# The third gate weight summed by ScalarE and rounded by GpSimd, and the next batch's input of the second attention in eight transfers

## The chip, the cores and the metric

One core of a Trainium2 chip. The metric is the device time in microseconds of one execution, in the median of several.

## The reference, cut to what matters

Two layers over the same 4 x 1024 tokens of width 256. Each takes a layer norm, an attention, and a gate network whose output, through silu, multiplies the attention's. The change touches the second layer alone: its gate network (the third weight, `w3`) and the order in which its attention loads its input.

```python
def _quantize(w):
    gamma = jnp.mean(jnp.abs(w))
    return jnp.clip(jnp.round(w / (gamma + 1e-08)), -1.0, 1.0)

x1 = x @ _quantize(w1).T            # w1, w2: 704 x 256, w3: 256 x 704
x2 = x @ _quantize(w2).T
hidden = jax.nn.sigmoid(x1) * x2
g = _silu(hidden @ _quantize(w3).T)

q, k, v = x @ Wq.T, x @ Wk.T, x @ Wv.T    # 32 heads of 64, rotary positions on q and k
# 30 heads look at the current block of 128 and the 64 rows before it, 2 heads at all rows before
x = x + (attention(q, k, v) @ Wo.T + bo) * g
```

## The kernel before

One program for all five engines, written out by hand: each stage has a plan, a Python list of steps, and every engine walks the same list and issues its own part of each step, in that order. An engine never overtakes: what waits holds back all that stands behind it on that engine. The stages before the change (the first layer, some 1460 us) aren't touched.

**The gate network** (`gate_network_plan`, `gate_network`) works on eight chunks of 512 tokens. A chunk has six steps `hidden` of 128 hidden units. TensorE makes two products into two PSUM banks (L1319, L1320: eight matmuls of 128x512 a step), ScalarE takes the sigmoid of the first (L1284, `n_sg`), VectorE multiplies (L1394, `n_hf`), ScalarE copies it rounded to the product's format (L1288, `n_hdh`), VectorE subtracts that for the low part (L1398, `n_hdl`, from `n_hf` and `n_hdh`). The steps share four banks, so the products of a step wait for the sigmoid and the multiply of the step two before. Beside them runs the front of the next chunk: `sums` on VectorE (L1350, L1353 and the variance L1355), the power -1/2 of it on GpSimd (L1252, `n_rs`), `begin` on VectorE (L1362, `n_xn`, which needs `n_rs`), and the transposes `turn0` and `turn1` on TensorE (L1305, they need `n_xn`). From the second chunk on, two steps `tail` (L1330, L1331) multiply the chunk before it by the rounded third weight `n_f3`.

The third weight, 128 x 1536 numbers a core (`n_raw3`), is rounded in a step `quantize` behind the first `hidden` of the second chunk, all of it on VectorE: the sum of the absolute values (L1374), a product with ones on TensorE that adds it over the partitions (L1311), the threshold (L1377, L1380, L1382), the comparison below (L1385) and the one above minus the first (L1387). The first attention rounds the other two weights, 128 x 1408 each, in another way: their sum is one ScalarE instruction (L1011), their rounding three GpSimd instructions (L982, L984, L986).

**The second attention** (`second_attention_plan`, `second_attention`) has 64 turns, 16 for each of the four batches of 1024 tokens. A turn handles two heads in two strides (the 16th of a batch, with the two global heads, in eight short ones). A stride begins with the scores on TensorE (L1921). Beside a turn's attention run the projections of the next turn (L107 to L109), for which the weights come in two turns ahead. All transfers are issued by SyncE, one after the other, in this order within a turn: the four `earlier` (L1734 to L1737, copies of values between partitions), `load_x` or `load_gx` if there is one, `load_w` (L1708 for q, L1709 for k), every other turn `load_v` (L1713), then the `rope` transfers (L1745, 16 a turn). `wo` (L1750, 512 KB, every fourth turn), and the stores and fetches of the output (L1758, L1768, L1769) lie ahead of `earlier`. ScalarE rounds the weights that have come in a step `w_high` (L1834), which waits for both of `load_w`; behind it in ScalarE's queue is a copy of values out of PSUM (L1846, `b_vv`) that frees a bank which the next scores (L1921) need.

`load_x` is two transfers of 1 MB (L1719): for the second batch in turn 1, for the third in turn 15, for the fourth in turn 31. In turn 47 `load_gx` (two of 1 MB) brings what the last batch's output is multiplied by and added to. Turns are counted from 0.

## Time and profile before

| | us |
|---|---|
| median of 3 runs | 3141.9 |
| lowest and highest of them | 3138.3, 3142.72 |
| the profiled execution's own time | 3153.16 |
| its span, first to last instruction | 3151.3 |
| PE busy | 3018.0 (96%) |
| DVE busy | 2118.1 (67%) |
| ACT busy | 1862.7 (59%) |
| POOL busy | 1013.5 (32%) |

The mean granted clock of TensorE is 0.985 of full speed. The profiled execution took 11 us more than the median of the others; sums are made against its time. "L1834" is a line of the kernel before; PE is TensorE, DVE VectorE, ACT ScalarE, POOL GpSimd, SPq the queue on which SyncE issues transfers. The gate network runs from 1460 to 1632 us, the second attention from there to the end.

### The profile page before, as it was taken

The page shows a single profiled execution, that of the slowest core. Times are in us where ns is not written, and L with a number is a line of the kernel's source. Part 1 is how long each engine was busy: PE and PEld are TensorE (multiplying, and loading weights), DVE is VectorE, ACT ScalarE, POOL GpSimd, SP SyncE. Part 2 cuts the span into 40 slices and gives each one's busy share as a digit, 9 for nine tenths or more (in the row PEclk, how much of TensorE's full clock was granted, in tenths as well). Part 3 has the DMA queues.
Part 4 walks back from the last instruction along what each step waited for, and adds up shares of the span by engine and source line. Part 5 has one row for each costly group of instructions (what it writes and reads, how often), then busy time and mean ns, then how long its engine had stood idle before and what let it go on. Part 6 is the DMA issues. An engine that isn't in the chain of part 4 may idle for free. (4 is left out here: it accounts for less than half of the span.)

```text
span 3151.3 us, 66387 instructions
## 1 busy us (share of the span) xinstructions
PE 3018.0 (96%) x23638; PEld 2264.8 (72%) x23638; DVE 2118.1 (67%) x5888; ACT 1862.7 (59%) x4638; POOL 1013.5 (32%) x1627
## 2 busy tenths in 40 slices
PE   7999999999999999997988999999999999999999
PEld 5888888853444444444877888788887888788887
DVE  5666666678999989984755555655556555565556
ACT  4666666647877777774445555455554555545553
POOL 0000000001100000001016566576655766566653
PEclk9999999988999999998999999999999999999999
DMA  4111111231332232202324434354343543344431
GB/s 150 48 48 48 48 48 41 61 69 31 81 48 55 46 73 35 42 4 89 115 59 111 104 94 99 96 128 103 84 117 87 119 103 93 93 115 110 97 89 44
DMA packets 296483, 246.35 MB, mean 78 GB/s; under 512 B 148956, under 2 KB 231516, under 8 KB 296028
## 3 DMA queue, kind: packets, MB, share of 16 engines
q1 hardware_dynamic: 296156, 242.11, 31.2%
q8 instruction: 191, 3.13, 0.4%
q14 instruction: 136, 1.11, 0.1%
HBM read 100.71 MB, written 44.04 MB: 46 GB/s over the span
## 5 line engine op out<-in xcount | busy, mean ns | idle before, releaser
L1853 ACT ACTIVATE b_pp<-b_pp,b_nm 128x192 f32<-128x192 f32 (+2 forms) x1024 | 472.9, 463 | 452.8 <-DVE b_nm L2020 371.3
L176 DVE TENSOR_REDUCE mx<-ps 128x2 f32<-128x1024 f32 x512 | 622.4, 1224 | 64.4 <-PE ps L167 51.9
L1007 ACT ACTIVATE a_pt<-ps 128x512 f32<-128x512 f32 x1024 | 555.9, 595 | 185.3 <-PE ps L1043 184.3
L1823 POOL TENSOR_SCALAR b_pp<-b_pp,b_rc 128x192 f32<-128x192 f32 x960 | 387.0, 425 | 384.8 <-DVE b_rc L2029 384.8
L2041 DVE COPY b_pt<-ps 128x384 f32<-128x384 f32 (+2 forms) x336 | 181.9, 555 | 317.1 <-PE ps L1942 301.8
L2020 DVE CUSTOM_DVE_ANT_0 b_pp<-ps,b_mk 128x192 f32<-128x192 f32 x960 | 276.3, 353 | 134.9 <-PE ps L1921 134.9
L797 DVE SCALAR_TENSOR_TENSOR f_yac<-ps,f_cw,f_yac 128x128 f32<-128x128 f32 x992 | 277.9, 343 | 125.4 <-PE ps L596 123.0
L596 PEld LDWEIGHTS ps<-w,f_sq 128*128 128x128 f32 x2048 | 265.1, 191 | 26.5 <-issue 6.0
L596 PE MATMUL ps<-w,f_sq 128*128 128x128 f32 x2048 | 270.1, 275 | 0.3
L1976 PE MATMUL ps<-b_wo,b_oT 128*128 128x256 f32 x1024 | 241.6, 380 | 3.7 <-ACT b_vv L1846 3.7
L1056 PE MATMUL ps<-a_pt,a_v 128*32 128x256 f32 x3072 | 242.9, 396 | 0.0
L1942 PE MATMUL ps<-ident,b_pp 128*128 128x128 f32 x1440 | 234.2, 273 | 2.7 <-DVE b_qp L1998 2.5
L990 POOL TENSOR_TENSOR a_s<-a_s,g 128x256 f32<-128x256 f32 x32 | 23.4, 730 | 573.9 <-DVE a_s L1114 573.9
L1921 PE MATMUL ps<-b_kp,b_qp 64*128 64x192 f32 x1920 | 189.9, 337 | 18.0 <-ACT b_vv L1846 10.2
L1976 PEld LDWEIGHTS ps<-b_wo,b_oT 128*128 128x128 f32 x1024 | 185.3, 190 | 25.3 <-ACT b_vv L1846 4.4
L1942 PEld LDWEIGHTS ps<-ident,b_pp 128*128 128x128 f32 x1440 | 177.8, 141 | 34.2 <-issue 3.7
L490 ACT ACTIVATE rl<-ps 128x512 f32<-128x512 f32 x256 | 151.7, 593 | 80.0 <-PE ps L109 75.5
L1846 ACT ACTIVATE b_vv<-ps 128x256 f32<-128x256 f32 x256 | 97.5, 381 | 169.1 <-PE ps L109 168.8
L1921 PEld LDWEIGHTS ps<-b_kp,b_qp 64*128 64x128 f32 x1920 | 154.7, 188 | 56.3 <-issue 56.3
L1995 DVE TENSOR_TENSOR b_qf<-ps,xt 128x512 f32<-128x512 f32 x256 | 174.2, 681 | 29.5 <-PE ps L109 29.5
L1853 ACT ACTIVATION_READ_ACCUMULATOR b_pp<-b_pp,b_nm 128x1 f32 x1024 | 191.3, 187 | 0.0
L1968 PE MATMUL ps<-b_pt,b_vv 128*64 128x128 f32 x960 | 189.6, 279 | 0.0
(282 smaller groups left out, 7335.9 us busy)
## 6 DMA issues: line engine op xcount, KB each, us to landing
b_rt<-b_qf SPq DMA_DIRECT2D x1024, 64.0 KB, 2.0
qk_parts<-f_aa SPq DMA_DIRECT2D x32, 512.0 KB, 2.7
v_rows<-f_va_ SPq DMA_DIRECT2D x16, 512.0 KB, 2.8
rl<-in_W1qT SPq DMA_DIRECT2D x64, 128.0 KB, 2.6
rl<-in_W1kT SPq DMA_DIRECT2D x64, 128.0 KB, 2.6
rl<-in_W1vT SPq DMA_DIRECT2D x32, 256.0 KB, 3.0
b_wo<-in_W1oT SPq DMA_DIRECT2D x16, 512.0 KB, 3.7
b_vs<-b_vv SPq DMA_DIRECT2D x60, 128.0 KB, 2.9
```

Of the source, the lines that this page charges most:

```text
L176: e.tensor_reduce(M["mx"][kh % 3][:, :, jt, h], P.pair(s), AX.X, ALU.max, negate=True).then_inc(P.free_sem(s), 1)
L596: m = e.matmul(P.ap(s)[:, i * 128:(i + 1) * 128], sq[d % 4][:, i * 128:(i + 1) * 128], M["w2"][:, s[2], :], start=True, stop=True)
L797: m = e.scalar_tensor_tensor(out=o, in0=src, scalar=by, in1=o, op0=ALU.mult, op1=ALU.add)
L1007: e.activation(pt[(4 * i + 2 * j + a) % 12][:, :], P.ap((*s, a)), ACT.Exp).then_inc(P.free_sem((*s, a)), 1)
L1056: m = e.matmul(P.ap(group)[32 * j:32 * j + 32, x], vs[b % 2][c][:, 4 * g + j, :], pt[(4 * i + j) % 12][:, x], start=c == half == 0, stop=c ...
L1823: m = e.tensor_scalar(x, x, r[:, 2 * u + h:2 * u + h + 1], 1.0, ALU.mult, ALU.mult)
L1853: e.activation(x, x, ACT.Exp, bias=nm[n % 4][:, c:c + 1], scale=-1.0, accum_out=sm[n % 4][:, c:c + 1]).then_inc(exp_done, 1)
L1921: m = e.matmul(scores(u, h), q[r, d:d + 128], kk[r, d:d + 192], start=True, stop=True)
L1942: m = e.transpose(P.ap(f)[:, c * 128:(c + 1) * 128], pp[n % 3][:, at:at + 128], ident[:, :])
L1968: e.matmul(o1, v[:, i + u, right + 64:right + 128], y[:, 2, :], start=u == 0, stop=False)
L1976: m = e.matmul(P.ap(s)[:, 0:256], oT[:, n % 2 * 4 + c, t * 128:(t + 1) * 128], wo[n % 2][:, c, :], start=c == 0, stop=c == 3)
L2020: m = e.tensor_tensor_reduce(out=weights(n, u, h), in0=scores(u, h), in1=mask, scale=-0.125, scalar=3e38, op0=ALU.add, op1=ALU.min, accum_ ...
```

## The change

**The weight.** The step `quantize` becomes three. `size`, behind the first `hidden` of the first chunk: ScalarE sums the absolute values in one instruction. `sum`, behind that chunk's fourth `hidden`: TensorE's product with ones and VectorE's threshold. `round`, behind its fifth: GpSimd halves the threshold twice and rounds in three instructions over 128x1536. VectorE keeps one instruction of 128x1.

**The input.** `load_x` of the next batch becomes eight transfers of 256 KB (a half of the tokens, one of two blocks of 128 of the width, high or low part), one in each of turns 2 to 9 of every batch but the last. `load_gx` becomes eight of 256 KB in turns 2 to 9 of the last batch. They stand where the two stood, between `earlier` and `load_w`. The count that the readers wait for grows from 32 to 128.

```diff
@@ -1138,8 +1138,7 @@
             p.append(("hidden", c, n))
-            if (i, n) == (1, 0):
-                p.append(("quantize",))
+            p += [(x,) for x, at in (("size", (0, 0)), ("sum", (0, 3)), ("round", (0, 4))) if at == (i, n)]
         if i:
         else:
@@ -1169,7 +1168,7 @@
                 n_tail += 1
-            elif s[0] == "quantize":
+            elif s[0] == "sum":
                 P.take(s, 0)
         fq = M["fq"]
@@ -1251,6 +1250,17 @@
                                     ALU.pow).then_inc(rstd_ready, 1)
+                elif s[0] == "round":
+                    src = raw[:, :, :].rearrange("p a b -> p (a b)")
+                    w.wait_ge(*P.emptied(("sum",)))
+                    e.tensor_scalar(thr[:, 1:2], thr[:, 0:1], -0.5, None, ALU.mult).then_inc(thr_ready, 1)
+                    e.tensor_scalar(thr[:, 0:1], thr[:, 0:1], 0.5, None, ALU.mult).then_inc(thr_ready, 1)
+                    w.wait_ge(thr_ready, 2)
+                    e.tensor_scalar(neg[:, :], src, thr[:, 1:2], None, ALU.is_lt).then_inc(is_neg, 1)
+                    e.tensor_scalar(src, src, thr[:, 0:1], None, ALU.is_gt).then_inc(is_neg, 1)
+                    w.wait_ge(is_neg, 2)
+                    e.tensor_tensor(f3[:, :, :].rearrange("p a b -> p (a b)"), src, neg[:, :],
+                                    ALU.subtract).then_inc(f3_ready, 1)
                 elif s[0] == "ahead":
                         w.wait_ge(M["w_high"], 1)
@@ -1271,6 +1281,11 @@
                     e.activation(xh[c % 2][:, h, :], P.ap(s), ACT.Copy).then_inc(xh_ready, 1)
+                elif k == "size":
+                    w.wait_ge(raw_in, 32)
+                    w.wait_ge(pads, 3)
+                    e.activation(neg[:, :], raw[:, :, :].rearrange("p a b -> p (a b)"), ACT.Abs,
+                                 accum_out=gam[:, 0:1]).then_inc(gamma, 1)
                 elif k == "ahead":
                     e.activation(M["wh"][0], M["raw"], ACT.Copy).then_inc(M["w_high"], 1)
@@ -1305,7 +1320,7 @@
                     m.then_inc(P.full_sem(s), 1)
-                elif k == "quantize":
+                elif k == "sum":
                     w.wait_ge(pads, 3)
                     e.matmul(P.ap(s)[:, 0:3], one[:, :], gam[:, :], start=True, stop=True).then_inc(P.full_sem(s), 1)
@@ -1368,24 +1383,10 @@
                                     ALU.subtract).then_inc(P.free_sem(s), 1)
-                elif k == "quantize":
-                    w.wait_ge(raw_in, 32)
-                    w.wait_ge(pads, 3)
-                    e.tensor_reduce(gam[:, 0:1], raw[:, :, :], AX.XY, ALU.add,
-                                    apply_absolute_value=True).then_inc(gamma, 1)
+                elif k == "sum":
                     w.wait_ge(*P.filled(s))
                                     ALU.add).then_inc(P.free_sem(s), 1)
-                    w.wait_ge(*P.emptied(s))
-                    e.tensor_scalar(thr[:, 1:2], thr[:, 0:1], -0.5, None, ALU.mult).then_inc(thr_ready, 1)
-                    w.wait_ge(thr_ready, 1)
-                    e.tensor_scalar(thr[:, 0:1], thr[:, 0:1], 0.5, None, ALU.mult).then_inc(thr_ready, 1)
-                    w.wait_ge(thr_ready, 2)
-                    src = raw[:, :, :].rearrange("p a b -> p (a b)")
-                    e.tensor_scalar(neg[:, :], src, thr[:, 1:2], None, ALU.is_lt).then_inc(is_neg, 1)
-                    w.wait_ge(is_neg, 1)
-                    e.scalar_tensor_tensor(out=f3[:, :, :].rearrange("p a b -> p (a b)"), in0=src, scalar=thr[:, 0:1],
-                                           in1=neg[:, :], op0=ALU.is_gt, op1=ALU.subtract).then_inc(f3_ready, 1)
                 elif k == "hidden":
                     w.wait_ge(*P.emptied((*s, 0)))
@@ -1512,12 +1513,10 @@
             p.append(("earlier", n))
-        if n == 1:
-            p.append(("load_x", 1))
-        if last and b + 2 < B:
-            p.append(("load_x", b + 2))
-        if last and b + 2 == B:
-            p.append(("load_gx", b))
+        if 2 <= at < 10 and b + 1 < B:
+            p.append(("load_x", b + 1, at - 2))
+        if 2 <= at < 10 and b + 1 == B:
+            p.append(("load_gx", b - 1, at - 2))
         if n + 2 < NTURN:
         if n % 2 == 0 and n + 4 < NTURN:
@@ -1663,7 +1662,7 @@
         def x_loaded(b):
-            return x_in[b % 2], 32 * ((b + 1) // 2)
+            return x_in[b % 2], 128 * ((b + 1) // 2)
 
 
@@ -1715,15 +1714,17 @@
                         w.wait_ge(*P.filled(("values", NP // 2 * (n - 2) + NP // 2 - 1, NQ - 1)))
-                    for h, x in enumerate((xh, xl)):
-                        e.dma_start(x[n % 2][:, :, :].bitcast(F32),
-                                    X["xT"][h, :, :, n * L:(n + 1) * L].rearrange("k p t -> p k t")).then_inc(x_in[n % 2], 16)
+                    half, kk, h = s[2] // 4, s[2] // 2 % 2, s[2] % 2
+                    r = slice(half * CH, (half + 1) * CH)
+                    e.dma_start((xh, xl)[h][n % 2][:, kk, r].bitcast(F32),
+                                X["xT"][h, kk, :, n * L + half * CH:n * L + (half + 1) * CH]).then_inc(x_in[n % 2], 16)
                 elif k == "load_gx":
                     w.wait_ge(*P.filled(("values", NP // 2 * n + NP // 2 - 1, NQ - 1)))
-                    for i, x in enumerate(("g2", "x1")):
-                        e.dma_start(gx_last[i], X[x][NTOK - L:NTOK, :].rearrange("(t p) d -> p t d",
-                                                                               p=128)).then_inc(gx_last_in, 16)
+                    i, t = s[2] // 4, s[2] % 4 * 2
+                    r = slice(NTOK - L + t * 128, NTOK - L + (t + 2) * 128)
+                    e.dma_start(gx_last[i][:, t:t + 2, :], X[("g2", "x1")[i]][r, :].rearrange(
+                        "(t p) d -> p t d", p=128)).then_inc(gx_last_in, 16)
                 elif k == "earlier":
                     w.wait_ge(*P.emptied(("values", n // 2, NQ - 1)))
@@ -1777,7 +1778,7 @@
             else:
-                w.wait_ge(gx_last_in, 32)
+                w.wait_ge(gx_last_in, 128)
                 by, to = gx_last[0][:, t, :], gx_last[1][:, t, :]
```

GpSimd's queue in the gate network, before: the powers of five chunks stand in a row, ahead of the second attention's first low parts.

```order
L1246 MEMSET n_one 128x128
L1247 MEMSET n_gam 128x3
L1252 TENSOR_TENSOR n_rs<-n_va,half 128x4 [waits n_var] x5
L1257 TENSOR_TENSOR w1b_l<-rl,w1b_h 128x256 [waits w_high]
L1260 TENSOR_TENSOR w1b_l<-rl,w1b_h 128x256 [waits v_high]
```

The same queue after the change (its line numbers are those of the changed file).

```order
L1245 MEMSET n_one 128x128
L1246 MEMSET n_gam 128x3
L1251 TENSOR_TENSOR n_rs<-n_va,half 128x4 [waits n_var] x2
L1256 TENSOR_SCALAR n_thr<-n_thr 128x1 [waits bank0_free]
L1257 TENSOR_SCALAR n_thr<-n_thr 128x1
L1259 TENSOR_SCALAR n_neg<-n_raw,n_thr 128x1536 [waits n_thr]
L1260 TENSOR_SCALAR n_raw<-n_raw,n_thr 128x1536
L1262 TENSOR_TENSOR n_f<-n_raw,n_neg 128x1536 [waits n_is_neg]
L1251 TENSOR_TENSOR n_rs<-n_va,half 128x4 [waits n_var] x3
```

The five instructions of the rounding stand behind the powers of the first two chunks and ahead of the third chunk's.

VectorE's queue at the start of the second chunk, before: the rounding of the weight stands between the low part of the chunk's first `hidden` and the third chunk's `begin`.

```order
L1355 TENSOR_SCALAR n_va<-n_mv 128x4
L1394 TENSOR_TENSOR n_hf<-ps,n_sg 128x512
L1398 TENSOR_TENSOR n_hdl<-n_hf,n_hdh 128x512
L1374 TENSOR_REDUCE n_gam<-n_raw 128x1
L1377 TENSOR_SCALAR n_thr<-ps 128x1
L1380 TENSOR_SCALAR n_thr<-n_thr 128x1
L1382 TENSOR_SCALAR n_thr<-n_thr 128x1
L1385 TENSOR_SCALAR n_neg<-n_raw,n_thr 128x1536
L1387 SCALAR_TENSOR_TENSOR n_f<-n_raw,n_thr,n_neg 128x1536
L1362 TENSOR_SCALAR n_xn<-g,n_mv,n_rs 128x256 x4
L1394 TENSOR_TENSOR n_hf<-ps,n_sg 128x512
```

The same queue after the change, from the start of the third chunk's `sums` to its `begin`.

```order
L1365 BN_STATS n_st<-g 128x6 x4
L1368 BN_AGGR n_mv<-n_st 128x2 x4
L1370 TENSOR_SCALAR n_va<-n_mv 128x4
L1395 TENSOR_TENSOR n_hf<-ps,n_sg 128x512
L1399 TENSOR_TENSOR n_hdl<-n_hf,n_hdh 128x512
L1377 TENSOR_SCALAR n_xn<-g,n_mv,n_rs 128x256 x4
L1395 TENSOR_TENSOR n_hf<-ps,n_sg 128x512
```

Nothing of the weight is left between them; the one instruction that stays, the threshold, stands a chunk earlier.

SyncE's queue in turn 1, before: both transfers of the second batch's input stand ahead of the weights that turn 3 needs.

```order
L1737 DMA b_vb<-b_vv 64x7x64
L1719 DMA b_xh<-xT_parts 128x2x1024
L1719 DMA b_xl<-xT_parts 128x2x1024
L1708 DMA rl<-in_W1qT 128x2x128
L1709 DMA rl<-in_W1kT 128x2x128
L1745 DMA b_rt<-b_qf 32x512 x16
```

After the change, from the end of turn 0's `rope` through turn 1 to the weights of turn 2.

```order
L1738 DMA b_vb<-b_vv 64x7x64
L1707 DMA rl<-in_W1qT 128x2x128
L1708 DMA rl<-in_W1kT 128x2x128
L1746 DMA b_rt<-b_qf 32x512 x16
L1735 DMA b_vs<-b_vv 64x7x64
L1736 DMA b_vs<-b_vv 64x8x64
L1737 DMA b_vb<-b_vv 64x8x64
L1738 DMA b_vb<-b_vv 64x7x64
L1719 DMA b_xh<-xT_parts 128x512
L1707 DMA rl<-in_W1qT 128x2x128
L1708 DMA rl<-in_W1kT 128x2x128
L1712 DMA rl<-in_W1vT 128x2x256
```

Turn 1 has no input left ahead of its weights, and turn 2 has one transfer of a quarter of the size, as have the turns after it.

## Rows read from the trace of the kernel before

**Rows 1.** Windows: us; busy us of PE, PEld, DVE, ACT, POOL; clock, DMA, GB/s.

```profile
1485.00:1505.00 20.00, 12.66 (x52) 10.01 (x51) 15.60 (x32) 6.66 (x12) 1.01 (x1) 0.83 0.99 326
1664.00:1700.00 36.00, 25.83 (x232) 22.46 (x231) 16.02 (x66) 15.38 (x55) 18.32 (x33) 0.86 0.49 129
2050.00:2349.00 299.00, 299.00 (x2535) 257.41 (x2535) 175.18 (x659) 167.96 (x597) 195.17 (x328) 1.00 0.44 104
```

**Rows 2.** Timeline, PE: start us, us, instruction [idle before <-releaser].

```profile
1492.77 0.56 PE L1311 MATMUL ps<-n_gam,n_one 128*128 128x3 f32 x2 [7.34 <-DVE n_gam L1374]
1493.19 0.77 PE L1319 MATMUL ps<-xh,fq 128*128 128x512 f32 x1
...
1496.72 0.40 PE L1319 MATMUL ps<-xh,fq 128*128 128x512 f32 x1
...
1498.59 0.60 PE L1305 MATMUL ps<-ident,n_xn 128*128 128x128 f32 x4
...
1505.06 0.28 PE L1330 MATMUL ps<-n_f,n_hdh 128*128 128x256 f32 x1
```

**Rows 3.** Timeline, DVE, the same stretch.

```profile
1482.49 0.68 DVE L1369 TENSOR_TENSOR xl<-ps,xh 128x512 fp32r<-128x512 f32 x1
...
1488.89 0.69 DVE L1394 TENSOR_TENSOR n_hf<-ps,n_sg 128x512 f32<-128x512 f32 x1
...
1496.73 1.38 DVE L1362 TENSOR_SCALAR n_xn<-g,n_mv,n_rs 128x256 f32<-128x256 f32 x4
```

**Rows 4.** Groups by line and form, POOL: xcount | busy us, mean ns | idle before.

```profile
L1252 POOL TENSOR_TENSOR n_rs<-n_va,half 128x4 f32<-128x4 f32 x8 | 8.1, 1012 | 103.0 <-DVE n_va L1355 103.0
...
L982 POOL TENSOR_SCALAR fq<-a_raw,a_thr 128x1408 fp32r<-128x1408 f32 x2 | 7.8, 3876 | 0.2
L984 POOL TENSOR_SCALAR a_raw<-a_raw,a_thr 128x1408 f32<-128x1408 f32 x2 | 7.7, 3842 | 0.2
...
L986 POOL TENSOR_TENSOR fq<-a_raw,fq 128x1408 fp32r<-128x1408 f32 x2 | 6.4, 3206 | 0.2
```

**Rows 5.** Timeline, all engines, rounding of another weight in the first attention.

```profile
768.62 0.16 DVE L1094 TENSOR_SCALAR a_thr<-ps 128x1 f32<-128x1 f32 x1 [0.42 <-PE ps L1061]
...
777.29 3.20 POOL L986 TENSOR_TENSOR fq<-a_raw,fq 128x1408 fp32r<-128x1408 f32 x1
...
779.14 1.38 DVE L186 TENSOR_TENSOR nm<-mx 128x16 f32<-128x16 f32 x1
```

**Rows 6.** Line L186, all of its instructions: ns min/median/max.

```profile
L186 DVE TENSOR_TENSOR nm<-mx x32: 174/176/1377, 672.0 to 1412.7; 128x16 f32<-128x16 f32 x32
```

**Rows 7.** Line L1011, ScalarE's sum of absolute values in the first attention.

```profile
L1011 ACT ACTIVATE fq<-a_raw x2: 1379/1380/1381, 762.1 to 819.2; 128x1408 fp32r<-128x1408 f32 x2
```

**Rows 8.** Timeline, all engines, turn 1 of the second attention.

```profile
1672.01 0.63 SPq L1719 DMA_DIRECT2D b_xh<-xT_parts  x1
...
1682.70 0.63 ACT L1834 ACTIVATE w1b_h<-rl 128x512 fp32r<-128x512 f32 x1 [8.94 <-DMA rl<-in_W1kT]
```

**Rows 9.** Timeline, PE, turn 1: scores of its second stride and of the next turn's first.

```profile
1683.96 2.93 PE L1921 MATMUL ps<-b_kp,b_qp 64*128 64x192 f32 x16 [8.46 <-ACT b_vv L1846]
...
1695.83 1.57 PE L1921 MATMUL ps<-b_kp,b_qp 64*128 64x192 f32 x16 [0.85 <-DVE b_kp L1998]
```

**Rows 10.** Waits, ACT, turns 2 to 9 of the last batch: us, times, longest.

```profile
ACT w1b_h L1834 <- DMA rl<-in_W1kT: 9.2, 6, 4.0
```

**Rows 11.** Timeline, ACT and PE: turn 19, then turn 52.

```profile
2096.79 0.63 ACT L1834 ACTIVATE w1b_h<-rl 128x512 fp32r<-128x512 f32 x1 [2.06 <-DMA rl<-in_W1kT]
...
2866.10 0.63 ACT L1834 ACTIVATE w1b_h<-rl 128x512 fp32r<-128x512 f32 x1 [3.98 <-DMA rl<-in_W1kT]
...
2867.36 1.57 PE L1921 MATMUL ps<-b_kp,b_qp 64*128 64x192 f32 x16 [1.76 <-ACT b_vv L1846]
```

**Rows 12.** Timeline, ACT, turns 11 and 12, without and with a transfer of 512 KB.

```profile
1895.58 0.63 ACT L1834 ACTIVATE w1b_h<-rl 128x512 fp32r<-128x512 f32 x1 [0.16 <-DMA rl<-in_W1kT]
...
1918.14 0.63 ACT L1834 ACTIVATE w1b_h<-rl 128x512 fp32r<-128x512 f32 x1 [1.03 <-DMA rl<-in_W1kT]
```

## The prediction

> **What bounds the kernel now.** The windows by stage come first: in the second attention's steady turns TensorE is busy for 299 of 299 us [rows 1], and what is added to its path there is added to the time. So I looked for stretches where it isn't busy, and for what ends each wait. There are two at which the change aims. In the gate network TensorE stands still for 7.34 us up to 1492.77, until VectorE has summed the third weight, and then makes eight matmuls in 3.53 us (1493.19 to 1496.72), the next eight in 1.87 [rows 2]; the granted clock of that window is 0.83 [rows 1]: after the pause it runs at 1.2 GHz instead of 2.4, until some 3.8 us after it began again. In turn 1 of the second attention ScalarE waits 8.94 us for weights queued behind 2 MB of the next batch's input [rows 8]; TensorE's scores wait 8.46 us behind it, and the first sixteen take 2.93 us instead of 1.57 [rows 9]. Third, the place where something is added: ScalarE's wait for the weights in turns 2 to 9 of each batch [rows 10 to 12].
>
> **The gate network.** Taken off VectorE: 1.75 us of sum, 2.84 us of rounding and three instructions on one column. If that were all, `begin` (L1362), at 1496.73 before [rows 3], could start at 1491.0, when the low part before it ends, and the transposes (L1305), which need it, with it: 5.5 us gained. But look what the order puts in its place: GpSimd's rounding stands ahead of the third chunk's power (L1252), on which `begin` waits. Its price is in the first attention: 3.88, 3.84 and 3.21 us for 1408 columns [rows 4], for 1536 that is 10.92 x 1.09 = 11.9 us. From the end of VectorE's threshold (768.78) to the end of the last (780.49) it took 11.71 us, 0.8 more than the three together [rows 5], so 12.7 us here.
>
> It starts when VectorE has made the threshold, which now stands just ahead of the `xl` at 1482.49 [rows 3]. ScalarE's sum costs 1.38 us for 1408 columns [rows 7], 1.5 here and 0.2 for reading the total; it stands where ScalarE has idle time, and delays the next multiply by 0.1 us at most, since VectorE is busy with `begin` of the second chunk until then. So the threshold is ready at 1482.7, GpSimd is done at 1495.4, its power (1.01 us, rows 4) at 1496.5, and `begin` starts at 1496.5, where it started before. The gain is gone; the wait has a new name.
>
> Two things make it a loss. First, the pause: TensorE does two more `hidden` steps and stands still from 1491 until the transposes at 1497.9. That is 7 us, as long as the pause that brought 1.2 GHz before. Before, the slow matmuls ran while VectorE rounded; now they come after `begin`, on the path. From the transposes at 1498.59 to the first `tail` at 1505.06 TensorE was never idle, 6.47 us of work [rows 2]. Starting at 1497.9 and with 3.8 us at half speed, 1.9 us lost, the tails begin at 1506.3: 1.2 us later. Second, GpSimd holds VectorE up. The maximum L186, with both inputs in SBUF, takes 0.176 us [rows 6], but 1.38 us when it began inside the last rounding instruction, and it ended at 780.52, 0.03 us after it [rows 5]. The low parts (L1398) also have both inputs in SBUF, and two of them fall into instructions of 4.2 us; so does the variance. By this the multiply that frees the bank of the next `hidden`, 1488.89 before [rows 3], comes at 1496.3, GpSimd is done at 1496.4, since it waits for the two low parts in turn, `begin` starts at 1498.3 and the transposes at 1499.7. A part of the cold stretch is then over already, with the products of 1497. The tails begin between 1506.3 and 1508.1. I take 2.4 us lost, nearer the upper end, because each long instruction catches one low part; bounds 1.2 and 3.1.
> The Trainium skill, "SBUF — State Buffer", section "SBUF: two separate sides", says that VectorE and GpSimd share a port pair which an instruction holds as "an exclusive lock, not a bandwidth split", for its whole length. By that rule, the trace agrees (0.03 us after the end); without it the loss would be 1.2 us and the sum 1.2 us lower.
> After the tails VectorE waits for TensorE in every chunk, so the loss is carried to the end of the stage.
>
> **Turn 1.** Without its two transfers, of 0.53 us each in SyncE's queue, the weights are issued 1.1 us earlier, and they land in the usual 2.6 instead of 8.94 us. ScalarE then frees the bank by 1676.4, and next late is VectorE's k part, which held the scores of the turn after by 0.85 us [rows 9]: it ends at 1676.3. So the scores start at 1676.4 instead of 1683.96, 7.6 us gained, and with no pause the 1.9 us of the slow clock are spared, less 0.1 for what I can't place. Gain 9.4 us; the lower bound is 7.6.
>
> In turns 15, 31 and 47 the same transfers are taken away and nothing is gained: the weights there landed 7 us before ScalarE came to them, and TensorE's idle time, 4.7 us in each, waits for others.
>
> **The 32 small transfers.** They stand ahead of `load_w` in turns 2 to 9 of each batch. Behind them in SyncE's queue wait the weights and the `rope` transfers; the latter land 1.4 us or more before GpSimd takes them in all steady turns, which covers them. The weights have less. A transfer of 512 KB (`wo`) ahead of them raises ScalarE's wait from 0.16 to 1.03 us, 0.87 more [rows 12], and 1.4 more in another such pair (turns 43 and 44). A new one is half as large: 0.53 us of issue, and 0.3 for its data, half of what remains of the mean of the two, 1.15. I take 0.85 us. Lower end 0.53, the issue alone. Upper end 1.35: the 2 MB of turn 1 made the landing 6.3 to 6.6 us later, an eighth of that is 0.8, with the issue 1.35.
>
> How much is covered? In turn 19 ScalarE waited 2.06 us and TensorE not at all; in turn 52 it was 3.98 and 1.76 [rows 11]. So 2.2 us of the wait are free (1.3 in turns 2 and 3, whose strides are shorter). In the turns concerned ScalarE waits 20 times, 4.7, 5.5, 7.3 and 9.2 us by batch (the last in rows 10), the long ones being 2.3 (turn 4), 2.1 (19), 2.0, 1.9, 2.0 (34 to 36), 1.7, 1.9 and 4.0 (50 to 52). With 0.85 more on each, what exceeds 2.2 is 0.95 + 0.75 + 0.65 + 0.55 + 0.65 + 0.35 + 0.55 + 0.85 = 5.3, and turns 2, 3 and 20 add 0.5: 5.8 us. With 0.53 it is 2.8, with 1.35 it is 12.
>
> **The sum.** 2.4 - 9.4 + 5.8 = -1.2 us. The profiled execution took 3153.16 us (span 3151.3 and 1.9 around it) and becomes 3152.0. That is 11.3 us above the median of 3141.9; since every term is a difference, the median becomes 3140.7. What a measurement of this kernel can tell from no change is about 0.2%, 6.3 us.
>
> **Rivals.** (1) The small transfers are nearly free: their issue falls into time in which SyncE would wait anyway, and ScalarE's wait grows by 0.2 us or less. Then they cost 0.6, and with the gate network at its lower bound the sum is -7.6, at 2.4 it is -6.4: 3134.9, faster. Against it: SyncE issues the nine transfers up to the weights without a gap, and the pairs of turns show 0.87 and more. (2) GpSimd is done with the rounding before the third chunk's variance is ready (1489): it would have to take 6.2 us, half of what it took for a smaller weight. Then the 5.5 us are gained, -5.5 - 9.4 + 5.8: 3132.8. (3) Slower: the DMA engines, 0.99 busy when the load is dense [rows 1], are full with copies and ropes of short rows, and a new transfer delays the weights by its issue, its data and a stalled issue (two of 1.3 and 1.4 us preceded turn 52's wait), 1.8 us together. By the same count that is 19.7 us, sum +12.7: 3154.6. It decides from 1.4 us a transfer. (4) The change doesn't do in turn 1 what it says: the four copies ahead are what holds the weights, and half of the wait stays: gain 4.7, 3145.4, still no difference.
> The Trainium skill, "DMA: Bandwidth & Descriptors", section "Bandwidth", asks to batch transfers to 1 MiB or more for three quarters of the peak, which speaks against eight of 256 KB and for (3). Here issues follow each other by 0.5 us while each takes over 2 us to land, so the fixed part overlaps; that is why (3) stays small.
>
> **Chances.** Forecast 0.65, (1) 0.13, (2) 0.05, (3) 0.13, (4) 0.04. Faster by over 0.2%: 0.18; within: 0.69; slower: 0.13. The forecast's own bounds are 1.2 - 9.4 + 2.8 = -5.4 and 3.1 - 7.6 + 12 = +7.5, 3136.5 to 3149.4. The range reaches down to (1) and leaves out (2), (3) and the very end where all bad bounds meet: 3134.0 to 3148.5.
>
> **What would show it.** The three rounding instructions on GpSimd of some 4.2, 4.2 and 3.5 us, ending near 1496; the power behind them and `begin` behind that at 1498; low parts on VectorE of 3 us instead of 0.69; a pause of TensorE of over 5 us before the transposes, then matmuls at half speed, and the first tail 1 to 3 us later than 1505. In turn 1 no wait of ScalarE over 1.5 us and scores at 10 us' distance. In turns 2 to 9 ScalarE's wait for the weights 0.85 us longer, and TensorE waiting for L1846's successor some ten times for 0.3 to 1 us. I am wrong if the powers don't wait for the rounding, if the weights land as early as before in spite of the transfer ahead, or if the wait grows by over 1.4 us.

## The result: 0.35% slower

The changed kernel takes 3150.49 us in the median of 22 runs (3145.9 to 3171.37), the kernel before 3142.26 in as many (3136.06 to 3152.15). The ratio is 1.0035, 95% interval 1.0024 to 1.0045, or +8.2 us by the medians. The forecast was 3140.7 with a range up to 3148.5.

The profiled execution of the changed kernel has a span of 3147.5 us at a mean clock of 0.991. The one of before (3151.3 at 0.985) was a long one: its gate network began 14 us later, behind stages that the change doesn't touch. So stages are compared from their own beginnings here, and since one trace of before is thin ground, a second one was taken (`h3_before_again`, below). "The gate stretch" is the time from the first `begin` to the first `tail`; from there the tails of all chunks took 123.2 us in every kernel.

| us | before | before, again | changed |
|---|---|---|---|
| gate stretch | 41.25 | 42.19 | 43.77 |
| first scores of the second attention to the end | 1502.88 | 1504.24 | 1510.31 |
| of it, gained up to turn 2's first scores | | | -9.0, -9.3 |
| of it, lost behind them | | | +16.5, +15.4 |

(The last two rows are differences to the one and to the other trace of before.)

**The gate network after.** VectorE, then GpSimd, from the fifth `hidden` of the first chunk on (start, us; line, operation; in brackets the idle time before it and who ended it). L1399 is the low part (L1398 before), L1370 the variance (L1355), L1377 `begin` (L1362).

```profile
1474.49 2.86 DVE L1399 TENSOR_TENSOR n_hdl<-n_hf,n_hdh 128x512 fp32r<-128x512 f32 x1 [0.70 <-ACT n_hdh L1303]
...
1478.58 0.36 DVE L1368 BATCH_NORM_AGGREGATE n_mv<-n_st 128x2 f32<-128x6 f32 x4
1478.98 2.23 DVE L1370 TENSOR_SCALAR n_va<-n_mv 128x4 f32<-128x4 f32 x1
...
1483.10 1.38 DVE L1377 TENSOR_SCALAR n_xn<-g,n_mv,n_rs 128x256 f32<-128x256 f32 x4
```

```profile
1469.34 4.19 POOL L1259 TENSOR_SCALAR n_neg<-n_raw,n_thr 128x1536 f32<-128x1536 f32 x1
...
1473.51 4.16 POOL L1260 TENSOR_SCALAR n_raw<-n_raw,n_thr 128x1536 f32<-128x1536 f32 x1
1477.76 3.42 POOL L1262 TENSOR_TENSOR n_f<-n_raw,n_neg 128x1536 fp32r<-128x1536 f32 x1
1481.29 1.03 POOL L1251 TENSOR_TENSOR n_rs<-n_va,half 128x4 f32<-128x4 f32 x1
```

And TensorE: the pause that [rows 2] showed ahead of L1311 stands now ahead of a `hidden` step, and ends when a multiply has freed its bank.

```profile
1481.85 0.79 PE L1334 MATMUL ps<-xh,fq 128*128 128x512 f32 x1 [5.66 <-DVE n_hf L1395]
...
1493.59 0.28 PE L1345 MATMUL ps<-n_f,n_hdh 128*128 128x256 f32 x1
```

The low part of 0.69 us takes 2.86 and ends 0.4 us before the last rounding instruction begins; the variance, 128x4 numbers, takes 2.23 instead of 0.17 and ends 0.03 us behind it. The power follows, and `begin` behind the power and a low part.

**The gate network's loss by parts.** `begin` of the third chunk starts 33.3 us behind the first `begin`, where it was 32.9: 0.4 us of the 2.5 us that are lost against the first trace. The other 2.2 us lie between this `begin` and the first tail. The windows of that stretch, before and after (us; busy us of PE, PEld, DVE, ACT, POOL; clock, DMA, GB/s):

```profile
1496.73:1505.06 8.33, 8.33 (x42) 6.78 (x40) 6.24 (x13) 4.32 (x8) 0.00 (x0) 1.00 0.95 334
```

```profile
1483.10:1493.59 10.49, 9.79 (x35) 7.51 (x34) 7.46 (x15) 5.25 (x10) 0.00 (x0) 0.67 0.81 289
```

Before, the clock was back at 2.4 GHz when `begin` started; now a large part of the stretch runs at 1.2. Traces of one and the same gate network differ in this too: the stretch took 9.25 us at a clock of 0.89 in the second trace of before, and 9.56 at 0.75 in `e1_weight`, which rounds as the changed kernel does.

**Turn 1 after.** ScalarE's rounding of the weights and TensorE's scores of the next stride; before, they had waited 8.94 and 8.46 us ([rows 8, 9]).

```profile
1663.15 0.63 ACT L1835 ACTIVATE w1b_h<-rl 128x512 fp32r<-128x512 f32 x1 [0.31 <-DMA rl<-in_W1kT]
```

```profile
1665.45 1.57 PE L1922 MATMUL ps<-b_kp,b_qp 64*128 64x192 f32 x16 [0.85 <-DVE b_kp L1999]
```

**The small transfers after.** Waits, from turn 2 to the end of the program: ScalarE for the k weights, and TensorE's scores for the copy of values that stands behind them in ScalarE's queue (us in all, times, longest). Before:

```profile
ACT w1b_h L1834 <- DMA rl<-in_W1kT: 39.3, 34, 4.0
...
PE ps L1921 <- ACT b_vv L1846: 1.8, 1, 1.8
```

After:

```profile
ACT w1b_h L1835 <- DMA rl<-in_W1kT: 80.6, 47, 4.4
...
PE ps L1922 <- ACT b_vv L1847: 17.0, 16, 2.2
```

The wait of ScalarE has doubled, and TensorE, which had waited once, waits 16 times. Turns 19 and 52 of ScalarE, which stood at 2.06 and 3.98 in [rows 11], and turn 51 of both engines:

```profile
2082.99 0.63 ACT L1835 ACTIVATE w1b_h<-rl 128x512 fp32r<-128x512 f32 x1 [3.30 <-DMA rl<-in_W1kT]
...
2837.51 0.63 ACT L1835 ACTIVATE w1b_h<-rl 128x512 fp32r<-128x512 f32 x1 [4.42 <-DMA rl<-in_W1kT]
...
2860.36 0.63 ACT L1835 ACTIVATE w1b_h<-rl 128x512 fp32r<-128x512 f32 x1 [3.29 <-DMA rl<-in_W1kT]
```

```profile
2838.77 1.57 PE L1922 MATMUL ps<-b_kp,b_qp 64*128 64x192 f32 x16 [2.20 <-ACT b_vv L1847]
```

### The profile page after: what moved, and what is told of

Its sections match the earlier page's. It is cut to its first block and busy times, and to the rows that moved or that the text cites. A ratio compares the mean times of both kernels' runs of the same rounds, so it can differ in the third digit from the quotient of the medians.

```text
span 3147.5 us, 66413 instructions
## 1 busy us (share of the span) xinstructions
PE 3006.3 (96%) x23638; PEld 2263.0 (72%) x23638; DVE 2119.5 (67%) x5883; ACT 1863.1 (59%) x4640; POOL 1025.7 (33%) x1632
```

## The experiments

The times are set against the kernel before. A table behind the experiments on the transfers holds the waits of all of them.

**One part at a time.** `e1_weight` takes only the hunks of the gate network, `e2_input` only those of the input.

> Only the third gate weight is treated as in the changed kernel; the input of the second attention is loaded as before. Theory: the rounding costs TensorE 2.5 us up to the first tail (43.8 us from the first begin to the first tail instead of 41.25) and the second attention is as before, so the time is 2.7 us above before (3145), ratio 1.0009. Rival (the gate part carries the whole loss by a way that the trace of the whole change hides, such as the clock): +8 us or more.

Measured: ratio 1.0006 (0.9995 to 1.0016), no difference that can be told. Gate stretch 42.85 us; the second attention 1502.30, as before.

> Only the input is loaded in eight transfers; the gate network is as before. Theory: turn 1 gives back 9.4 us, the 32 small transfers ahead of the weights cost 15 to 17, the sum is +7 (ratio 1.002). Scores of turn 1 come 7.6 us earlier, and ScalarE's wait for the weights in the turns concerned sums to about 65 us instead of 26.9. Rival (small transfers cost little, the loss is elsewhere): -6 or less.

Measured: 1.0020 (1.0008 to 1.0032), some 6 us slower. Turn 1 gains 7.6 us, and ScalarE waits 65.3 us in turns 2 to 9 of the four batches instead of 26.9 (33.0 in the second trace of before). The larger loss is in the input, as expected; the rivals of both runs are out.

**The place in the queue.** `e3_behind` is the changed kernel with the eight transfers behind the weights of their turn.

```diff
-        if 2 <= at < 10 and b + 1 < B:
-            p.append(("load_x", b + 1, at - 2))
-        if 2 <= at < 10 and b + 1 == B:
-            p.append(("load_gx", b - 1, at - 2))
         if n + 2 < NTURN:
             p.append(("load_w", n + 2))
         if n % 2 == 0 and n + 4 < NTURN:
             p.append(("load_v", n // 2 + 2))
+        if 2 <= at < 10 and b + 1 < B:
+            p.append(("load_x", b + 1, at - 2))
+        if 2 <= at < 10 and b + 1 == B:
+            p.append(("load_gx", b - 1, at - 2))
```

> The changed kernel with the eight small transfers of each batch moved behind load_w and load_v of their turn. Theory (the place in the queue costs: what stands ahead of the weights makes them late): ScalarE's waits in the turns concerned fall back to some 27 to 32 us in sum, the cost of the small transfers to 0 to 2 us, the time is 14 us below the changed kernel and 4 to 6 us below before (3137). Rival (the DMA engines are shared, and data costs wherever it stands): landing of the k weights stays at 3.2 instead of 2.7 us, the cost stays at 5 us or more, 3143 or above.

Measured: 3135.7 us, ratio 0.9973 (0.9962 to 0.9984), faster than before. From turn 2 on:

```profile
ACT w1b_h L1835 <- DMA rl<-in_W1kT: 51.6, 36, 3.8
...
PE ps L1922 <- ACT b_vv L1847: 3.0, 4, 1.6
```

The same bytes in the same turns, and ScalarE waits 29 us less. The second attention is 13.9 us shorter than in the changed kernel. One expectation was missed: in turns 2 to 9 the waits sum to 36.5 us, not 27 to 32. In four later traces with the transfers in the same place (`g1_early` to `g4_dve_split`) they sum to 28 to 29. The k weights land 2.9 us after their issue, against 3.3 in the changed kernel and 2.7 and 2.8 in the two traces of before, so the rival's late landing isn't there.

**The size.** `e4_tiny` and `e5_64k` are the kernel before with one more transfer ahead of the weights in turns 2 to 9 of three batches; it writes again 8 KB, or 64 KB, that are already there.

```diff
+        if 2 <= at < 10 and b + 1 < B:
+            p.append(("again", b + 1))
...
+                elif k == "again":
+                    e.dma_start(xh[n % 2][:, 0, 0:16].bitcast(F32),
+                                X["xT"][0, 0, :, n * L:n * L + 16]).then_inc(x_in[n % 2], 16)
```

> The kernel before with one extra transfer of 8 KB ahead of the weights in turns 2 to 9 of the first three batches (it writes again what is there). It tells the price of an issue from that of the data. If the issue alone costs: ScalarE's waits of those turns rise by 0.5 us where they were over 0.3, landing of the k weights stays at 2.7 us, and TensorE loses 3 us in all. If a transfer costs by its being there whatever its size: 1.3 us a turn and 10 us or more in the three batches.

> e4_tiny with the extra transfer of 64 KB instead of 8 KB. If the price is the issue and, in proportion, the data (0.38 us more wait for 8 KB, 1.4 for 256 KB, against the kernel before): 0.6 us more wait. If the wait depends on the number of transfers alone: 0.4 us. If any block of full rows costs the same: 1.3 us.

Measured: ScalarE's wait for the k weights from turn 2 on, for 8 KB and for 64 KB:

```profile
ACT w1b_h L1839 <- DMA rl<-in_W1kT: 53.5, 42, 3.0
```

```profile
ACT w1b_h L1839 <- DMA rl<-in_W1kT: 58.9, 41, 4.2
```

These sums run over the whole stage and differ by 11.5 us between traces that have nothing extra in those turns (39.3, 46.3, 50.8), so the price is read from the 24 turns concerned alone. There ScalarE waits 17.6 us in the first trace of before, 22.2 in the second and 22.1 in `e1_weight`; 26.6 with 8 KB, 28.9 with 64 KB, 45.7 with the changed kernel's 256 KB. That is 0.2 to 0.4 us for each transfer of 8 KB, 0.3 to 0.5 for one of 64 KB and 1.0 to 1.2 for one of 256 KB. The landings say the same: the k weights land 8.1, 8.3 and 8.3 us after the turn's first scores with nothing extra, 8.5 and 8.6 with 8 and 64 KB, 9.3 with 256 KB. SyncE's run of issues up to the weights grows by 0.5 to 0.6 us in all three, but behind the 8 KB the weights land sooner after their issue (2.39 us in the mean of these turns, against 2.71), and behind 256 KB later (3.21). So an issue alone costs little and the data is most of the price; how little, the spread of the traces doesn't tell. Against the first trace of before, on which the expectation was built, the rises in turns that had waited are 0.38 and 0.61 us, as it said; against the second they are 0.16 and 0.27. From turn 2 on the stage loses 0.7 to 1.7 us by the 8 KB, where 3 had been said.

**Where it costs.** `f2_quiet_ahead` is `e2_input` with the transfers still ahead of the weights, but in turns 5, 6, 7 and 9 to 13 of each batch.

```diff
-        if 2 <= at < 10 and b + 1 < B:
-            p.append(("load_x", b + 1, at - 2))
+        quiet = (5, 6, 7, 9, 10, 11, 12, 13)
+        if at in quiet and b + 1 < B:
+            p.append(("load_x", b + 1, quiet.index(at)))
...
```

> e2_input (gate network as before, small transfers ahead of the weights) with the transfers in turns 5, 6, 7 and 9 to 13 of each batch. Theory (a transfer delays the weights by 1.3 us in any turn, and costs only what exceeds the 2.2 us that are free): ScalarE's waits rise by about as much per turn, but TensorE loses only in turns 12, 44, 60 and their like, 1 to 3 us in all instead of 15; the second attention ends 7 to 8 us earlier than before. Rival (each transfer costs TensorE by its being there): 10 us or more, no gain.

Measured:

```profile
ACT w1b_h L1835 <- DMA rl<-in_W1kT: 80.4, 55, 3.1
...
PE ps L1922 <- ACT b_vv L1847: 3.8, 6, 0.9
```

ScalarE waits as long as in the changed kernel, 80.4 us against 80.6, and TensorE 3.8 instead of 17.0: the wait as such costs nothing, what stands over the cover costs. The second attention takes 1497.25 us, 5.6 and 7.0 us less than in the two traces of before (7 to 8 were expected). Of what was lost behind turn 1, 1.0 us came in turn 28 and 0.9 in turn 60, both of the kind that was named, and 0.7 in turn 17, where nothing was changed.

**What the pair with `wo` had hidden.** Two more, for the step of the prediction that had failed: `h1_front` puts the small transfers of `e2_input` ahead of the four copies `earlier`, where `wo` stands; `h2_512k` makes four transfers of 512 KB of them, in turns 2, 4, 6 and 8.

```diff
+        if 2 <= at < 10 and b + 1 < B:
+            p.append(("load_x", b + 1, at - 2))
+        if 2 <= at < 10 and b + 1 == B:
+            p.append(("load_gx", b - 1, at - 2))
         if not last:
             p.append(("earlier", n))
-        if 2 <= at < 10 and b + 1 < B:
-            p.append(("load_x", b + 1, at - 2))
-        if 2 <= at < 10 and b + 1 == B:
-            p.append(("load_gx", b - 1, at - 2))
```

> e2_input with the small transfers ahead of the four copies between partitions instead of behind them, so that 2.6 us of other issues stand between them and the weights. If the distance decides (the data has left the DMA engines when the weights are issued): ScalarE's wait rises by 0.3 to 0.6 us a turn where it waited before instead of 1.4, its sum in turns 2 to 9 is 35 to 42 us instead of 65, the second attention ends 5 us or more earlier than in e2_input (1503 from its first scores instead of 1508). If any transfer ahead costs the same: 65 us and 1508.

> e2_input with half as many transfers of twice the size (512 KB, in turns 2, 4, 6 and 8 of each batch), immediately ahead of the weights. If the price goes with the bytes: in those turns the wait rises by 2.4 to 2.7 us, in the others not at all, and TensorE loses as much as in e2_input or more (only half as many turns have the cover of 2.2 us). If it is a price for each transfer: 1.3 us in those turns.

> The kernel before once more. The first trace has 26.9 us of ScalarE's waits in turns 2 to 9 and 41.25 us from the first begin to the first tail, the waits of the kernels that do the same there are 28 to 31 us. Expected 27 to 31 us, and 41 to 42.2 us in the gate network.

Measured: `h1_front` lies between its two expectations. The distance helps by a quarter, not by two thirds: the wait is 56.7 us in turns 2 to 9, where 35 to 42 or 65 had been said. The second attention takes 1503.15 us, as the first of them said, since TensorE waits 4.3 us less than in `e2_input`. For 512 KB the wait rises by 1.67 us in the mean of the turns concerned that had waited (against the second trace of before), and not in the others; 256 KB cost 1.05 there by the same count. Both expectations, 2.4 to 2.7 us by the bytes and 1.3 by the transfer, were missed: the price goes with the bytes, but less than in proportion. TensorE loses more than in `e2_input`: 1516.10 us. The second trace of before has 33.0 us of waits in turns 2 to 9, a little more than expected, and 42.19 us in the gate stretch.

| | extra, ahead of the weights | wait of ScalarE | TensorE's scores behind it | second attention | from turn 2's first scores on |
|---|---|---|---|---|---|
| before | none | 39.3 | 1.8 | 1502.88 | 1455.5 |
| before, again | none | 50.8 | 1.6 | 1504.24 | 1456.6 |
| e1_weight | none | 46.3 | 1.3 | 1502.30 | 1455.7 |
| e4_tiny | 24 of 8 KB | 53.5 | 3.2 | 1502.69 | 1457.2 |
| e5_64k | 24 of 64 KB | 58.9 | 7.1 | 1509.76 | 1463.0 |
| e3_behind | none (32 behind them) | 51.6 | 3.0 | 1496.44 | 1458.0 |
| h1_front | 32 of 256 KB, further ahead | 73.3 | 11.5 | 1503.15 | 1465.3 |
| changed | 32 of 256 KB | 80.6 | 17.0 | 1510.31 | 1472.0 |
| e2_input | the same | 81.1 | 15.8 | 1508.15 | 1469.8 |
| h2_512k | 16 of 512 KB | 77.1 | 18.7 | 1516.10 | 1478.1 |
| f2_quiet_ahead | 32 of 256 KB, other turns | 80.4 | 3.8 | 1497.25 | 1458.9 |

(Waits from turn 2 to the end. Of the kernels ahead of `e3_behind` in the table, turn 1 is as before; the last column leaves it out, and is what compares them all.)

**The slow clock behind the short pauses.** Some rows of the table don't add up by waits alone: in `h2_512k` TensorE's scores wait 1.7 and 2.9 us longer than in the changed kernel and in `e2_input`, and the stage is 5.8 and 8.0 us longer. The windows of two turns of the changed kernel (us; busy us of PE, PEld, DVE, ACT, POOL; clock, DMA, GB/s), the first with a pause of 2.01 us at its head:

```profile
1684.19:1706.34 22.15, 19.29 (x165) 16.65 (x164) 11.34 (x46) 12.40 (x44) 14.14 (x24) 0.92 0.41 96
1706.34:1728.39 22.05, 19.89 (x182) 17.38 (x181) 13.18 (x49) 11.96 (x43) 12.96 (x23) 1.00 0.52 130
```

The granted clock of the first is 0.92: a part of it ran at 1.2 GHz instead of 2.4, which cost 1.6 us on top of the pause. In `h2_512k` the same is seen three times, behind pauses of 2.26 us (turn 2, clock 0.92), 1.96 (turn 4) and 2.17 (turn 52, 0.93 in both), each with 1.6 us lost on top; `e2_input` has no such stretch. That makes up for nearly all of the 8.0 us. In `e5_64k` it is seen behind a pause of 1.94 us (turn 36, clock 0.93), where 3.3 of its 7.1 us above `e4_tiny` were lost. It isn't certain: of the nine pauses from 1.94 to 2.26 us behind turn 1, in all the traces, four left the clock at 1.00, namely 2.20 us in turn 51 of the changed kernel, 2.06 and 2.20 in turns 2 and 3 of `e2_input`, and 1.98 in turn 3 of `h1_front`. The length of the pause alone doesn't decide; what does is not shown.

**The gate network.** Four kernels move the rounding; all stand on `e3_behind`, whose gate stretch is 43.79 us. `g1_early` makes the threshold and the rounding two and three steps sooner, `g2_late` the rounding two steps later, behind the third chunk's power. `g3_dve` gives the rounding back to VectorE, at its old place, and `g4_dve_split` does so in two pieces, in the first chunk.

```diff
-("size", (0, 0)), ("sum", (0, 3)), ("round", (0, 4))
+("size", (0, 0)), ("sum", (0, 1)), ("round", (0, 1))
```

```diff
-("size", (0, 0)), ("sum", (0, 3)), ("round", (0, 4))
+("size", (0, 0)), ("sum", (0, 3)), ("round", (1, 0))
```

```diff
-("size", (0, 0)), ("sum", (0, 3)), ("half", (1, 0)), ("round", (1, 0))
+("size", (0, 0)), ("sum", (0, 2)), ("half", (0, 3)), ("round", (0, 5))
```

(The last is `g4_dve_split` against `g3_dve`; "half" is the threshold's halves and the comparison below, "round" the comparison above minus the first, both on VectorE.)

> As e3_behind, but the threshold and GpSimd's rounding stand two steps earlier (behind the second hidden step of the first chunk), so that the rounding is over before the third chunk's variance. The stretch from the first begin to the first tail was 43.8 us in e3_behind. Theory Q (the loss is the power queued behind the rounding): 38 to 39.5, since the power comes 4 us earlier. Theory L (the loss is that each of GpSimd's three long instructions holds one or two VectorE instructions up, wherever it stands): three holds of some 2 us again, 42 to 43.5.

> As e3_behind, but the rounding stands behind the third chunk's power, one step later. Q: begin no longer waits for it, only the first tail does; rounding from the power's end (some 29 us from the first begin) for 12 us, first tail at 41.5 to 42.5. L: the holds fall on the second chunk's low parts, and the stretch is 43.5 or more.

> As e3_behind, but the rounding is VectorE's again, in the place of the kernel before (behind the second chunk's first hidden step); ScalarE still makes the sum. No GpSimd instruction is long any more. L and Q both expect that VectorE has 1.75 us less to do than before and TensorE's pause is that much shorter: first tail 38.5 to 39.8 us after the first begin (41.25 before). Rival: the pause still costs the slow clock and the tail is not before 40.5.

> As g3_dve, but the rounding's two long instructions stand apart, behind the fourth and the sixth hidden step of the first chunk. If VectorE's work is what bounds these two chunks the stretch is as in g3_dve; if the one long pause costs more by the slow clock behind it, two short ones cost less: 37 to 38.5 us.

Measured, gate stretch: 42.58, 48.60, 41.12 and 39.55 us. `g1_early` decides between the two theories. The power no longer waits for the rounding, and yet little is gained, for three low parts are held instead (VectorE, L1399, 0.69 us when free):

```profile
1464.12 3.18 DVE L1399 TENSOR_TENSOR n_hdl<-n_hf,n_hdh 128x512 fp32r<-128x512 f32 x1 [0.70 <-ACT n_hdh L1303]
...
1469.20 2.26 DVE L1399 TENSOR_TENSOR n_hdl<-n_hf,n_hdh 128x512 fp32r<-128x512 f32 x1 [0.70 <-ACT n_hdh L1303]
...
1473.35 2.55 DVE L1399 TENSOR_TENSOR n_hdl<-n_hf,n_hdh 128x512 fp32r<-128x512 f32 x1 [0.70 <-ACT n_hdh L1303]
```

In `g2_late` the rounding met `begin`, four VectorE instructions from SBUF to SBUF that take 1.38 us together. They took 12.28, until the rounding was over. VectorE, then GpSimd:

```profile
1478.26 12.28 DVE L1377 TENSOR_SCALAR n_xn<-g,n_mv,n_rs 128x256 f32<-128x256 f32 x4
1490.46 0.68 DVE L1395 TENSOR_TENSOR n_hf<-ps,n_sg 128x512 f32<-128x512 f32 x1
```

```profile
1477.92 4.49 POOL L1259 TENSOR_SCALAR n_neg<-n_raw,n_thr 128x1536 f32<-128x1536 f32 x1
1482.39 4.18 POOL L1260 TENSOR_SCALAR n_raw<-n_raw,n_thr 128x1536 f32<-128x1536 f32 x1
1486.65 3.42 POOL L1262 TENSOR_TENSOR n_f<-n_raw,n_neg 128x1536 fp32r<-128x1536 f32 x1
```

TensorE's pause was 12.48 us. The 48.60 us are above what Q said (41.5 to 42.5) and fall under L's "43.5 or more", though another instruction was held than the low parts that L named. `g3_dve` came out as its rival said: VectorE has 1.75 us less to do, TensorE's pause is 4.73 us instead of 7.34, but the slow matmuls now come behind the pause on the path, and the tail comes no sooner (41.12). With two pauses of 1.84 and 1.60 us instead of one, `g4_dve_split` is 1.6 us better, though 1 us short of what was expected. The two later traces of this same gate network (`f1_quiet_behind` and `f3_split_behind`, below) have 39.74 and 40.53 us, each with a pause of 3.14 us, so what is gained over `g3_dve` is between 0.6 and 1.6 us; why, these traces don't settle.

**A version that beats both.** The kernel of `g4_dve_split` (sum on ScalarE, rounding on VectorE in two places, transfers behind the weights) was timed again as `f3_split_behind`, beside `f1_quiet_behind`, which has the quiet turns of `f2_quiet_ahead` too.

> The kernel of g4_dve_split again, timed in rounds beside f1: 3131 to 3133, ratio 0.9965.

> g4_dve_split (weight's sum on ScalarE, rounding on VectorE in two places; small transfers behind the weights), and the small transfers stand in turns 5, 6, 7 and 9 to 13 of each batch, where ScalarE waited least for the weights, instead of 2 to 9. Theory: gate network 4 us shorter than in e3_behind, small transfers cost 0 to 1 us instead of 3: 3129 to 3132, ratio 0.996. Rival (the rest of the cost of the small transfers doesn't depend on the turn): no better than g4 with the transfers in turns 2 to 9, 3131 to 3133.

Measured: 3128.58 us, ratio 0.9955 (0.9940 to 0.9970), and 3131.44, 0.9966 (0.9955 to 0.9977). The two intervals overlap, and the second attention took 1495.22 and 1495.32 us: behind the weights, no difference is seen between these two choices of turns. Both beat the kernel before by 11 to 14 us.

## Why the prediction was wrong

It failed in one term of the sum, the small transfers, and the sign went with it.

- **The gate network: right in size, in part by luck.** By its steps, counted from the first `begin`: threshold 18.9 forecast, 18.9 measured; end of the rounding 31.6 to 32.6, 31.4; `begin` of the third chunk 32.7 to 34.5, 33.3; first tail 42.5 to 44.3, 43.8. Forecast 2.4 us lost; 2.5 against the first trace, and 1.7 when the three kernels with GpSimd's rounding (43.77, 42.85, 43.79) are set against the eight with the old gate network (41.15 to 42.19, mean 41.8). That VectorE would be held was right, and it is why `begin` gained nothing: `g1_early` shows that the order in GpSimd's queue, which the prediction put first, isn't what costs. But of the loss itself only 0.4 us is a later `begin`; 2.2 us lie behind it, where the matmuls run at the slow clock, which the prediction had named and taken too short. It had 3.8 us at 1.2 GHz behind the pause, read from the first trace of before (3.9); the changed kernel had 8.1, `e1_weight` 6.1, the second trace of before 5.9. The Trainium skill, "SBUF — State Buffer", section "SBUF: two separate sides", gives the lock also to a VectorE instruction in a two-port mode with one input; `begin` in `g2_late`, 12.28 us for 1.38, is an instruction with one tensor as its input that was held; in which mode it ran no run shows. The four aggregates of `sums` (L1368, 0.36 us, in the midst of the last rounding instruction of the changed kernel) were not held.
- **Turn 1: right.** 7.6 us less wait ahead of its scores, as forecast, and with the clock's share behind it 9.0 and 9.3 us by turn 2's first scores; against the first trace 0.4 of it was lost again in turn 0, by chance. Forecast 9.4.
- **Turns 15, 31 and 47: right.** The stage's difference doesn't move there (0.03 us or less in each).
- **The small transfers: wrong in size.** This is the step that failed. Forecast 5.8 us, upper bound 12; measured 16.5 and 15.4 us behind turn 2's first scores, by the two traces of before. Three things are in it. First, the price of one: 0.85 us forecast, 1.33 measured in the 18 turns of the first trace that had waited over 0.3 us (1.0 in 23 turns, against the second trace). The 0.53 for the issue held: the weights are issued 0.5 us later (0.7 against the first trace). The 0.3 for the data was too small: they also land 0.5 us later after their issue, 3.21 us instead of 2.7. The row it came from, turns 11 and 12 [rows 12], shows 512 KB with 3.6 us of other issues between it and the weights. `h1_front` shows that such a distance takes a quarter off the price, not more; what the rest is stays open. Second, the first trace of before was a lucky one: 39.3 us of waits against 46.3 and 50.8 in two kernels that do the same there. Waits close under the edge of the cover were read from it as if they were fixed. Third, a pause of 2 us can cost 1.6 us more by the slow clock; the prediction had charged that only to the long pause of turn 1.
- **The cover: right.** 2.2 us of ScalarE's wait are free; `f2_quiet_ahead` has the same wait as the changed kernel and a quarter of the loss.

With 1.35 us in place of 0.85, its own upper end, the prediction's count gives 12 us, and the sum +5; with the slow clock of turn 2 it is +6.6, where +8.2 was measured. The stages of the traces give +10.0 (2.5 - 9.0 + 16.5) and +7.7 (1.6 - 9.3 + 15.4). Its rival (3) named the sign and the weights delayed by issue and data, with the price too high (1.8 us, +12.7): the stalled issue that it added isn't in the 0.5 to 0.6 us by which SyncE's run of issues grew. Its point of decision, 1.4 us, was close. That bound of 1.35 us was worked out from turn 1, the one row in which input stood immediately ahead of the weights, as these transfers do; that row deserved more weight than the pair that looked cleaner.

The Trainium skill, "DMA: Bandwidth & Descriptors", section "Issuing engines are not separate DMA queues", calls the sequencer's time to start a transfer "usually small relative to the DMA itself". The runs agree: SyncE took 0.6 to 0.7 us in the median to issue a small transfer, and it landed 3.3 to 4.1 us after that. The rule of the same page to batch to 1 MiB, cited in the prediction for its rival (3), points to the wrong remedy here: half as many transfers of twice the size made the second attention 8 us longer (`h2_512k` against `e2_input`), 2.9 us of it longer waits and most of the rest the slow clock behind three of them.

## What to carry to other kernels

When a transfer is added, look at what stands directly behind it in the same queue: its bytes delay that transfer more than its issue does. Put what isn't urgent behind what is; the same 32 transfers cost 13 to 16 us ahead of the weights (`e2_input` and the changed kernel) and 2.5 us or less behind them. And work given to GpSimd isn't off VectorE's path if both read SBUF: here each long GpSimd instruction held up the next VectorE instruction of that kind until it was over or within 0.4 us of it, however small that one was.

## What the runs showed that was not expected

- A VectorE step of 1.38 us took 12.28 because it met three GpSimd instructions in a row (`g2_late`): one of the four instructions got through at a time.
- Behind an extra transfer of 8 KB the weights landed 0.3 us sooner after their issue, so that the issue in front cost 0.2 to 0.4 us and not its own 0.5 to 0.6.
- Of nine pauses of TensorE of 1.94 to 2.26 us, five were followed by a granted clock of 0.92 or 0.93 over the turn and four by 1.00.
- Behind the pause of the gate network the clock stayed at 1.2 GHz for 3.9 us in one trace of the kernel before and for 5.9 in the other, and its gate stretch is 41.25 us in the one and 42.19 in the other.
- The waits of one and the same program differ between executions by more than the effect that was being costed: 39.3 and 50.8 us in two traces of the kernel before.
